# Value tiles turned by DMA and VectorE, and a shorter chain for the keys' coefficient, in a gated delta-rule layer with routed experts

## The reference, cut to what matters

```
mixed = silu(causal_conv(xn @ W_qkv))            # 8 key heads, 16 value heads, 128 wide, 4 taps
q, k, v = split(mixed);  z = xn @ W_z
beta = sigmoid(xn @ W_b);  g = -exp(A_log) * softplus(xn @ W_a + dt_bias)
q = l2norm(q) / sqrt(128);  k = l2norm(k)        # each key head serves two value heads
for each token:  S = S * exp(g);  S = S + k (beta * (v - k S))^T;  o = q S
s = (rms_norm(o) * norm_weight * silu(z)) @ W_out
ffn: the two experts with the largest summed logits, for all tokens, w1 -> gelu -> w2, mixed by softmax
```

## Time and profile before

| | us |
|---|---|
| median of 3 executions | 2076.18 (2070.57 to 2081.19) |
| the profiled execution: time | 2080.1 |
| the profiled execution: span | 2078.3 |
| TensorE busy | 2008.6 (97%) |
| VectorE busy | 1353.6 (65%) |
| ScalarE busy | 909.1 (44%) |
| GpSimd busy | 834.1 (40%) |

### The profile page before, as it was taken

The page is one execution under the profiler, slowest core; times in us unless marked ns, Lnnn a source line. Parts: engine busy times, 40 slices in busy tenths (PEclk is TensorE's granted clock), DMA queues, the critical chain, the costliest instruction groups (busy, mean ns, idle before and its releaser), DMA issues.

```text
span 2078.3 us, 39559 instructions
## 1 busy us (share of the span) xinstructions
PE 2008.6 (97%) x13730; PEld 1713.5 (82%) x13730; DVE 1353.6 (65%) x3169; ACT 909.1 (44%) x2525; POOL 834.1 (40%) x2123
## 2 busy tenths in 40 slices
PE   5789999999999999999999999999999999999999
PEld 3578888888888888888888888888888888887887
DVE  6868877778688878787777445555555444446442
ACT  4555555555465555556555532222223232233221
POOL 1456666666575766666565511100010210101111
PEclk9889999999999999999999999999999999999999
DMA  4233545343535444434443232443334434303441
GB/s 125 51 74 79 97 84 100 79 96 80 89 84 94 92 97 81 97 81 97 88 87 71 77 93 59 94 92 81 77 76 92 118 86 99 69 26 122 152 143 70
DMA packets 388022, 184.25 MB, mean 89 GB/s; under 512 B 249456, under 2 KB 369136, under 8 KB 385776
## 3 DMA queue, kind: packets, MB, share of 16 engines
q1 hardware_dynamic: 354640, 177.73, 37.8%
q10 hardware_dynamic: 33184, 4.01, 1.3%
HBM read 135.26 MB, written 46.40 MB: 87 GB/s over the span
## 4 chain that ended last, share of the span: by engine, by line
PE 69%; issue 10%; DVE 6%; DMA 5%; POOL 4%; ACT 3%; SPq 2%; ACTq 0%; POOLq 0%; DVEq 0%
PE bank L333 17%; PE bank L335 17%; PE bank L334 17%; DMA VT<-v_dram 4%; PE bank L565 3%; PE bank L574 2%; PE bank L548 2%; PE bank L468 2%; PE bank L584 2%; PE bank L556 2%; PE bank L527 2%; PE bank L533 1%; POOL y_out L1823 1%; POOL V L1771 1%; POOL prod L1769 1%
## 5 line engine op out<-in xcount | busy, mean ns | idle before, releaser
L1769 POOL TENSOR_TENSOR prod<-A_in,V 128x60 f32<-128x60 f32 (+24 forms) x992 | 301.4, 304 | 269.6 <-DMA A_in<-a_dram 199.3
L1771 POOL TENSOR_TENSOR V<-V,prod 128x60 f32<-128x60 f32 (+24 forms) x992 | 311.1, 314 | 77.8
L1098 ACT ACTIVATE hid<-bank,bias 128x512 f32<-128x512 f32 x128 | 88.3, 690 | 455.3 <-PE bank L335 453.5
L1813 POOL TENSOR_TENSOR ffn_w_lo<-ffn_raw,ffn_w_hi 128x1024 fp32r<-128x1024 f32 x32 | 77.9, 2437 | 470.3 <-ACT ffn_w_hi L1088 466.4
L1563 DVE TENSOR_TENSOR h_lo<-hid,h_hi 128x512 fp32r<-128x512 f32 x128 | 91.1, 712 | 265.8 <-ACT h_hi L1105 265.8
L1577 DVE SCALAR_TENSOR_TENSOR gate_acc<-bank,rw,gate_acc 128x512 f32<-128x512 f32 x240 | 177.6, 748 | 58.8 <-PE bank L335 58.8
L333 PE MATMUL bank<-ffn_w_hi,h_hi 128*128 128x512 f32 x512 | 199.3, 389 | 1.2 <-DVE h_lo L1563 1.0
L333 PE MATMUL bank<-xn_hi,ffn_w_hi 128*128 128x512 f32 x512 | 200.3, 391 | 0.0
L335 PE MATMUL bank<-xn_hi,ffn_w_lo 128*128 128x512 f32 x512 | 199.2, 389 | 0.0
L334 PE MATMUL bank<-xn_lo,ffn_w_hi 128*128 128x512 f32 x512 | 199.2, 389 | 0.0
L335 PE MATMUL bank<-ffn_w_hi,h_lo 128*128 128x512 f32 x512 | 199.2, 389 | 0.0
(11 more groups left out here) (224 smaller groups left out, 5178.0 us busy)
## 6 DMA issues: line engine op xcount, KB each, us to landing
E<-eg_dram SPq DMA_DIRECT2D x64, 256.0 KB, 8.1
A_in<-a_dram SPq DMA_DIRECT2D x32, 512.0 KB, 4.0
decb<-dec_dram SPq DMA_DIRECT2D x128, 128.0 KB, 4.2
og_dram<-og SPq DMA_DIRECT2D x64, 256.0 KB, 2.2
ffn_raw<-w SPq DMA_DIRECT2D x32, 512.0 KB, 4.0
og_x<-og_dram SPq DMA_DIRECT2D x256, 64.0 KB, 2.7
ogT_dram<-og_y SPq DMA_DIRECT2D x64, 256.0 KB, 2.4
og_in<-ogT_dram SPq DMA_DIRECT2D x16, 1024.0 KB, 5.2
```

The lines of the kernel that those rows point to most:

```text
L1098: act.activation(hid[:, i % 2, :], bank[i % 4][:, :], ACT.Gelu_apprx_tanh, bias=bias1[:, k, f * NF + ft:f * NF + ft + 1]).then_inc(S_["gel ...
L1769: pool.tensor_tensor(prod[:, 0:m, 0:n], column, V[:, vb, 0:m, j:j + 1].to_broadcast([P, m, n]), MUL).then_inc(S_["product"], 1)
L1771: pool.tensor_tensor(V[:, vb, 0:m, j + 1:B32], V[:, vb, 0:m, j + 1:B32], prod[:, 0:m, 0:n], ADD).then_inc(S_["solve_step"], 1)
L1813: pool.tensor_tensor(fw[m, "lo", n % 2][:, :], raw[:, i % 2, :], fw[m, "hi", n % 2][:, :].bitcast(f32), SUB).then_inc(S_["ffn_lo"], 1)
```

## The change

It moves the transposition of the value tile from TensorE to DMA and VectorE. SyncE's new `load_v(b)` waits for both halves of `vS` and issues 16 DMAs, each of one 32x32-blocked square of all eight (head, chunk) pairs: 32 partitions x 8 pieces of 128 bytes, from `vS` to a new tile `v_x`, so that block (i, j) stands where block (j, i) was. VectorE's new `turn_v(b)` then transposes inside the 32x32 blocks, one instruction of 128x512 for each head, into `v_tok`, which now has one buffer. `put_v` multiplies `v_tok` in place. The chain for the coefficient becomes: (norm + epsilon) times -(1 + exp(-b)), kept as `neg_inv`, then one reciprocal; `c_rem` and norm + epsilon are made once a block, in `key_remains`, after the pairs. Other waits are renumbered.

```diff
-        neg_beta = alloc(att, "neg_beta", [NT, HEADS])
+        neg_inv = alloc(att, "neg_inv", [NT, HEADS])
...
-        v_tok = alloc(p2b, "v_tok", [2, CPS, REP * HD])
+        v_tok = alloc(p2b, "v_tok", [REP, CPS, HD])
+        v_x = alloc(p2b, "v_x", [REP * CPS, P])
...
             def project_v0(st):
                 if is_block(st - 1):
-                    pe.wait_ge(S_["v_tok"], 2 * st)
+                    pe.wait_ge(S_["z_gate"], CPS * (st - 1) + 3)
...
             def turn_k(st):
                 b = st - 1
-                pe.wait_ge(S_["v_tok"], 2 * b + 1)
+                if is_block(st):
+                    pe.wait_ge(S_["CP"], CPS * (st + 1))
+                else:
+                    pe.wait_ge(S_["k_rem"], b)
...
-            def turn_v(st, half):
...
-                for i in range(2):
-                    c = 2 * half + i
-                    for h in range(REP):
-                        r = pe.transpose(TV_BANK[half][:, (REP * i + h) * P:(REP * i + h + 1) * P], vS[:, h, c * P:(c + 1) * P], C["ident"])
-                r.then_inc(S_["v_turned"], 1)
...
             def silu(b, kind):
...
-                        act.wait_ge(S_["v_turned"], 2 * b)
+                        act.wait_ge(S_["v_x"], V_X * b)
...
             def put_v(st, half):
-                act.wait_ge(S_["v_turned"], 2 * b + half + 1)
+                act.wait_ge(S_["v_turned"], b + 1)
...
-                if b >= 2:
-                    act.wait_ge(S_["R"], CPS * (b - 1))
                 for i in range(2):
                     c = 2 * half + i
-                    r = act.mul(v_tok[:, b % 2, c, :], TV_BANK[half][:, i * REP * HD:(i + 1) * REP * HD], roots[:, b % 4, c:c + 1])
+                    r = act.mul(v_tok[:, :, c, :], v_tok[:, :, c, :], roots[:, b % 4, c:c + 1])
...
                 if chain:
                     mean_squares(st - 2, 3)
                 if turned:
+                    put_v(st, 0)
                     put_y64(st - 1)
+                    put_v(st, 1)
...
             def gate_series(p):
-                dve.tensor_scalar(beta[:, r, :], beta[:, r, :], 1.0, None, ADD).then_inc(S_["beta"], 1)
-                dve.wait_ge(S_["beta"], 4 * p + 2)
-                dve.reciprocal(beta[:, r, :], beta[:, r, :]).then_inc(S_["beta"], 1)
-                dve.wait_ge(S_["beta"], 4 * p + 3)
-                dve.tensor_scalar(neg_beta[:, r, :], beta[:, r, :], -1.0, None, MUL).then_inc(S_["beta"], 1)
+                dve.tensor_scalar(neg_inv[:, r, :], beta[:, r, :], -1.0, -1.0, MUL, ADD).then_inc(S_["beta"], 1)
...
             def key_norms(st, half):
-                dve.tensor_scalar(norms[:, bb, r2], norms[:, bb, r2], L2_EPS, None, ADD).then_inc(S_["nk_eps"], 1)
-                dve.wait_ge(S_["nk_eps"], n)
-                dve.reciprocal(inv_n[:, r2], norms[:, bb, r2]).then_inc(S_["inv_n"], 1)
-                dve.wait_ge(S_["inv_n"], n)
-                dve.tensor_tensor(c_neg[:, bb, r2, :], neg_beta[:, cg, h0:h0 + REP],
-                                  inv_n[:, r2].rearrange("p (c o) -> p c o", o=1).to_broadcast([P, 2, REP]), MUL).then_inc(S_["c_neg"], 1)
+                dve.scalar_tensor_tensor(c_neg[:, bb, r2, :], norms[:, bb, r2].rearrange("p (c o) -> p c o", o=1).to_broadcast([P, 2, REP]), L2_EPS,
+                                         neg_inv[:, cg, h0:h0 + REP], ADD, MUL).then_inc(S_["nk_beta"], 1)
+                dve.wait_ge(S_["nk_beta"], n)
+                dve.reciprocal(c_neg[:, bb, r2, :], c_neg[:, bb, r2, :]).then_inc(S_["c_neg"], 1)
                 dve.wait_ge(S_["c_neg"], n)
-                dve.tensor_tensor(c_rem[:, bb, r2, :], c_neg[:, bb, r2, :], remain[:, cg, h0:h0 + REP], MUL).then_inc(S_["c_rem"], 1)
+
+            def key_remains(st):
...
+                dve.tensor_tensor(c_rem[:, bb, :, :], c_neg[:, bb, :, :], remain[:, cg, h0:h0 + REP], MUL).then_inc(S_["c_rem"], 1)
+                dve.tensor_scalar(norms[:, bb, 0:CPS], norms[:, bb, 0:CPS], L2_EPS, None, ADD).then_inc(S_["nk_eps"], 1)
...
+            def turn_v(b):
+                dve.wait_ge(S_["v_x"], V_X * (b + 1))
+                if b:
+                    dve.wait_ge(S_["R"], CPS * b)
+                for h in range(REP):
+                    r = dve.transpose(v_tok[:, h, :, :], v_x[:, h * CPS:(h + 1) * CPS, :])
+                r.then_inc(S_["v_turned"], 1)
...
                     pairs(st, 2)
                     pairs(st, 3)
+                    key_remains(st)
...
                 if chain:
                     chain_S(st - 2, 3)
+                if turned:
+                    turn_v(st - 1)
                 if now:
                     convolve(st, "v0")
...
             def lengths(b):
-                pool.wait_ge(S_["nk_eps"], 2 * b + 2)
+                pool.wait_ge(S_["nk_eps"], b + 1)
...
+            def load_v(b):
+                sp.wait_ge(S_["act_v0"], b + 1)
+                sp.wait_ge(S_["act_v1"], b + 1)
+                if b:
+                    sp.wait_ge(S_["v_turned"], b)
+                vf = vS[:, :, :].rearrange("p h t -> p (h t)").rearrange("p (m t) -> p m t", t=P)
+                for to in range(NQD):
+                    for at in range(NQD):
+                        r, q = slice(to * B32, (to + 1) * B32), slice(at * B32, (at + 1) * B32)
+                        sp.dma_start(v_x[r, :, q], vf[q, :, r]).then_inc(S_["v_x"], 16)
...
                 next_decay(2)
                 next_decay(3)
+                if turned:
+                    load_v(st - 1)
```

More of the change, by code:

```diff
@@ L75 @@
 ffn_bias ffn_bias1 ffn_raw0 ffn_raw1 wo_raw og_raw0 og_raw1 og_turned0 og_turned1 og_in0 og_in1 og_in2 x_res0 x_res1 out0 out1
-rows_out eg0 eg1 dec0 dec1 begin0 begin1 a_out a_in v_out vt_in
+rows_out eg0 eg1 dec0 dec1 begin0 begin1 a_out a_in v_out vt_in v_x
 xT smallT ab_turned sums score_parts scores_sum rows_turned
-proj_k proj_q proj_v0 proj_v1 z_proj k_turned q_turned v_turned pair_kq keys queries solved state_add out_add lev_y32 lev_z32 lev_y64 lev_z64
+proj_k proj_q proj_v0 proj_v1 z_proj k_turned q_turned pair_kq keys queries solved state_add out_add lev_y32 lev_z32 lev_y64 lev_z64
 sw_hi xn_hi ab_T ab_in exp_steps exp_sum rows
-tap_k tap_q tap_v0 tap_v1 act_k act_q act_v0 act_v1 carry_k carry_q carry_v0 carry_v1 z_gate q_sq k_rem v_tok U squares y32 z32 y64 inv w_hi
+tap_k tap_q tap_v0 tap_v1 act_k act_q act_v0 act_v1 carry z_gate q_sq k_rem v_tok U squares y32 z32 y64 inv w_hi
 softplus_steps router_steps stats var shift xn xn_lo beta softplus router rows_zero
-conv_k conv_q conv_v0 conv_v1 nk nk_eps inv_n c_neg c_rem q_eps CP E V_diag S_zero R S ms og w_lo_kq
+conv_k conv_q conv_v0 conv_v1 nk nk_eps nk_beta c_neg c_rem q_eps CP E v_turned V_diag S_zero R S ms og w_lo_kq
 half_pow rstd sw_lo k_len qd factor product solve_step w_lo_vz
@@ L148, in build @@
         p2 = ExitStack()
-        inv_n = alloc(p2, "inv_n", [CPS])
+        alloc(p2, "gap_n", [CPS])
         c_rem = alloc(p2, "c_rem", [4, CPS, REP])
@@ L249, in build @@
         KQ_BANK = (WORK_C, WORK_C)
-        TQ_BANK, TK_BANK, TV_BANK = WORK_B, WORK_C, (WORK_C, WORK_B)
+        TQ_BANK, TK_BANK = WORK_B, WORK_C
         def is_block(b):
@@ L316, in build @@
         CONV = 3
+        V_X = 16 * NQD * NQD
         SOLVES = B32 - 1
@@ L633, in attention_step @@
                 if turned:
-                    turn_v(st, 1)
                     turn_k(st)
@@ L663, in up_part @@
                     pe.wait_ge(S_["z_gate"], CPS * NU)
-                elif k == 0 and i == 1:
-                    pe.wait_ge(S_["v_tok"], 2 * NU)
                 elif k == 0 and i == 2:
@@ L767, in tensor @@
             project_z(1, 1)
-            turn_v(1, 0)
             project_q(1)
             project_z(1, 2)
-            turn_v(1, 1)
             turn_k(1)
@@ L859, in split_weights @@
                 act.copy(w_hi[kind][:, :, part * P:(part + 1) * P], w_raw[:, n % 2, :, :]).then_inc(S_["w_hi"], 1)
+            carries = 0
             def tap(b, kind):
+                nonlocal carries
+                carries += 1
                 gr, sb = b // NSB, b % NSB
@@ L1032, in attention_step @@
                     mean_squares(st - 2, 1)
-                if turned:
-                    put_v(st, 0)
                 if ahead:
@@ L1046, in attention_step @@
                 if turned:
-                    put_v(st, 1)
                     put_k(st)
@@ L1195, in scalar @@
             put_z(1, 1)
-            put_v(1, 0)
             exponents(3)
@@ L1200, in scalar @@
             put_z(1, 2)
-            put_v(1, 1)
             put_k(1)
@@ L1209, in scalar @@
             rates(3)
+            put_v(1, 0)
+            put_v(1, 1)
             for st in range(2, NU + 2):
@@ L1420, in chain_R @@
                     r = dve.scalar_tensor_tensor(R[:, h, :], bank[K_BANK][:, h * HD:(h + 1) * HD], decay[:, cg, h0 + h:h0 + h + 1],
-                                                 v_tok[:, b % 2, i, h * HD:(h + 1) * HD], MUL, SUB)
```

(5 more changed lines are left out.)

29 lines of the change are left out of this document (10 added, 19 removed).

## The result

The changed kernel takes 2244.4 us (median of 4 runs, 2239.6 to 2259.2), the kernel before 2076.0: 1.0824 times as long, with a 95% interval of 1.0764 to 1.0883. I had forecast 2101.5 us with a range up to 2132. The side was right, the size was wrong by a factor of seven: about 170 us are lost, not 25. The changed kernel and the experiments ran on different chips; the kernel before took 2076.0 us on the first and 2066.6 to 2068.6 on the others.

What follows compares the result with a forecast made beforehand. TensorE was taken to bound the attention stage. Terms -28.2 + 35.5 + 14 + 4 = +25.3 us on the profiled 2080.1 gave 2105.4, or 2101.5 us for the median, 1.2% slower; range 2081 to 2132.

Steps and rivals of the forecast that it cites:

- The likeliest case: Attention stage: transposes before `turn_q` and a tile late in 7 steps make the kernel slower, 2101.5 us; chance 0.46.
- VectorE waits 0.6 to 3.3 us ... 7 x 2.0 = +14 us: Seven steps with two weight loads in front: VectorE waits for the late tile, `turn_q` behind it, +14 us.
- in 22 steps the tile comes between 2.9 us early and 0.2 late: I take no delay: Steps without weight loads in front: the tile lands about when VectorE needs it, no delay counted.
- The time of issue: SyncE's `load_v`: 0.49 us for each of 16 transfers, 7.8 us a batch, 6.6 to 10.2 possible.
- late in nearly every step, by 1.0 us in 22 and 3.5 us in 7: Rival: at 0.64 us an issue behind a full queue, 46.5 us instead of 14, 2134 us; chance 0.20.
- TensorE without `turn_v`, -28.2: TensorE in the attention stage: eight transposes a block removed, 0.88 us each block, 32 blocks, -28.2 us.
- The two transposes on VectorE, +35.5: VectorE before `convolve(v0)`: 1.40 us for the pair, less slack, stalls the next step's `turn_q`, +35.5 us.
- `join_y32`, +4: TensorE at `join_y32`: `VT` comes later than TensorE does, about 0.6 us in each of 8 steps, +4 us (0 to 7).
- paid back: Rival: the `turn_q` stall replaces waiting at `join_y32`, at most 22.3 us, so faster, 2061 us; chance 0.07.
- The norm part: VectorE's norm operations: 0.5 us less a block with gaps, within VectorE's own slack; `CP` ready about 0.45 us earlier.
- `put_v`: ScalarE: its four 478 ns instructions now stand around `put_y64`, hidden; bound 0 to 0.3 us a step.
- The transfers as traffic: DMA engines under `load_v`: 4096 pieces a block are 3.3 us, so the 16 engines are no limit.

Runs made afterwards that it cites:

- e12: Changed kernel with the value tile not turned at all: no transfers, no transposes, ScalarE scales the unturned tile; 2053.2 us, 0.9919 of before.
- e3: Changed kernel without the transfers, VectorE's two transposes kept and reading straight from `vS`; 2092.3 us, 1.0118 of before.
- e13: e3 with VectorE's transposes made twice, still no transfers; 2164.2 us, 1.0460 of before.
- e14: e3 with VectorE's transposes made three times, still no transfers; 2248.2 us, 1.0865 of before.
- e1: Kernel before with only the norm part of the change, `turn_v` left on TensorE; 2061.1 us, 0.9962 of before.
- e2: Changed kernel with the norm part undone, value tile still turned by DMA and VectorE; 2241.9 us, 1.0839 of before.
- e15: e12 with all 16 transfers a block issued by SyncE but not awaited by VectorE for a turn; 2057.1 us, 0.9946 of before.
- e9: Changed kernel, whole, with 8 of each block's 16 transfers issued by SyncE and 8 by ScalarE; 2107.7 us, 1.0185 of before.

## Why the prediction was wrong

**The mechanism was the right one, its size was not.** The likeliest case said: slower, since VectorE's work goes in front of `turn_q` and the tile comes late. Both are seen. The step that failed is the term "VectorE waits 0.6 to 3.3 us ... 7 x 2.0 = +14 us", and with it "in 22 steps the tile comes between 2.9 us early and 0.2 late: I take no delay". By the chain e12, e3, after it is worth 146 us. Two things are wrong in it:

- *The time of issue.* I took 0.49 us for each of 16, from the four `VT` issues of the earlier trace rows, "0.41 to 0.64 possible". Measured: 0.61 for the median one, and some that stand longer, up to 2.4 us, so 10.9 to 14.5 us for a batch (median 12.4) instead of 7.8. From the batch's start to VectorE being ready for the tile there were 11 to 13 us in most steps and 7 to 9 in the eight with the longest waits, about what I had reckoned (12.3 and 8.8), and the tile was there 1.3 us behind the last issue in most steps, earlier than my 1.9: it is the issue alone that was too short. The upper bound held the median but not the batch, since I added the queue's standing still only before the batch and not within it. That a full queue is what holds SyncE was my reading of the 4.80 us in the earlier trace rows; no run here tests it. So the tile is late in all 30 steps, 1.0 to 3.2 us in 22 of them and 4.5 to 5.9 in the others, which are the seven with two weight loads and the last. My rival "late in nearly every step, by 1.0 us in 22 and 3.5 us in 7" had the place right but was too low as well.
- *The clock, which was in no term.* I priced a stall at its length. The earlier trace rows show 0.99, and I carried it over as if it could not change. With the waits it is 0.91, and the value projection's matmuls take 100 ns more each. e13 and e14 show, without any transfer, that this follows from the stall and about doubles the price of a microsecond above the first 1.4. Had I used 0.64 us an issue and this doubling, the rival's 46.5 would have become 93, and the forecast about 2180: still short, but outside the range that I gave.

**The other terms.** *TensorE without `turn_v`, -28.2*: measured -8 to -9 (e12 against e1). I counted the transposes' whole time as the bound's because TensorE was busy there; four of them in fact filled a wait for `S`. It is the second wrong term, hidden in the result by the first. *The two transposes on VectorE, +35.5*: 39 to 41 us of time (e3 against e12), 690 ns each (669 in e3) against the 695 of the earlier trace rows: right, though the wait at `turn_q` that the table names is only 24.6 us. *`join_y32`, +4*: its idle time fell, from 8.9 us to 5.1 at L500, one of my signs of a wrong forecast: TensorE comes later by the stall. (In e2, without the norm part, it is 2.3 us, so the stall is enough for that.) The 22.3 us of the earlier trace rows, from which I priced the rival "paid back", count the waits of the weight loads together with those of the matmuls; TensorE's own idle time there is the 8.9, and the rival's time would have been 2075 and not 2061. *The norm part*: counted as hidden, worth 8 us alone. *`put_v`*: hidden when the tile is on time. *The transfers as traffic*: hidden, 4 to 6 us (e15 against e12). By the ratios the measured terms are -8 for the norm part (e1), -9 (e12 against e1), +41 (e3 against e12) and +146 (the whole against e3), together +170 us. They must add up, since each is the step from one run to the next; what the runs show is how the sum is shared out.

**The signs.** 64 transposes of 0.69 us: as said. TensorE idle before `turn_q` 30 to 50 us: 107.5. Waits for `v_x` about 14, wrong above 40: 88.2. TensorE's own busy sum less by 28 to 39 us: it rose from 2008.6 to 2062.5 us with 256 instructions less, since more of them ran at half clock.

**The issue time against the rule that I had cited.** The Trainium skill's page "DMA: Bandwidth & Descriptors", section "Issuing engines are not separate DMA queues", says that issuing DMAs from several engines saves only the sequencer's time to start them, which is usually small relative to the DMA itself. Here that time was the term that decided: 0.61 us of SyncE for each, and giving half of them to ScalarE took 132 us off (e9).

**A version better than both.** e1, the norm part alone, is 0.38% faster than the kernel before. No whole version with the value tile turned by DMA reached it; e12's 2053 us says that at most 8 us more were there to be had. No run starts the 16 transfers earlier in SyncE's order, so whether they could be made early enough that way is open.

## What to carry to other kernels

- Before work is taken off the bounding engine, ask which wait it was covering: here 28 us of transposes were worth 8, since half of them stood in front of an instruction that would have waited for another engine. A run with the work simply left out gives the ceiling before the replacement is built.
- Many small transfers were priced here by their number on the issuing queue, one after the other, and counted from when the queue gets to them; the last one sets when the tile is there. Split them over two queues or make fewer of them.
- A stall of TensorE of a few microseconds in every step was not paid at its length here, but at up to twice of it. Look at the granted clock at each such stall in the trace of before (it is where the longest steps are) and count the matmuls behind it at the lower clock.

## What was not expected of the hardware

- The granted clock fell during stalls of `turn_q` or right behind them, and the first 1.4 us a step did not do it (0.989 in e3 against 0.989 in e12), the next 1.4 did (0.965) and the third more (0.937). I can't tell from these runs at what length of stall it begins; other waits of the step count as well.
- An issue of an SBUF to SBUF transfer takes SyncE 0.61 us (median) with 256 pieces and 0.60 with 128.
- In the kernel before three steps are longer than the others, near 401, 541 and 1087 us; each has a wait for `V_diag` and a stretch at half clock behind it. The effect was in the trace that I read. (There are such stretches also at 142, 1142 and 1173 us, near the two ends of the stage.) Stretches of the kernel before, columns as in the first table:

```profile
398.00:412.00 14.00, 12.30 (x158) 10.83 (x159) 11.04 (x34) 6.29 (x24) 7.45 (x20) 0.88 0.18 45
538.00:552.00 14.00, 10.92 (x152) 9.83 (x153) 9.48 (x31) 4.86 (x15) 5.94 (x16) 0.88 0.29 72
1084.00:1098.00 14.00, 12.24 (x158) 10.61 (x157) 9.82 (x31) 5.60 (x17) 7.42 (x22) 0.88 0.13 38
```

There the clock is 0.88 in the mean, where the whole attention stage has 0.99.
